# Packing products set one by one between the products of a half chunk

## The chip, the cores and the metric

The kernel runs on one core of a Trainium2 chip. The metric is the device time of one execution in microseconds, as the median of several runs. The engines that matter here are TensorE (PE in the rows, PEld for its weight loads), VectorE (DVE), ScalarE (ACT), GpSimd (POOL) and the DMA queue of SyncE (SPq).

## The reference

A graph attention layer and a graph averaging layer run over the same dense 0/1 adjacency matrix of 8192 x 8192 int32, with 8192 rows of 128 features.

```
Wh = h @ W
e = (Wh @ a1)[:, None] + (Wh @ a2)[None, :]
e = where(e > 0, e, 0.2 * e);  e = where(adj > 0, e, -9e15)
h_prime = softmax(e, axis=1) @ Wh
x = layernorm(x + elu(h_prime))
x1 = adj @ x / deg
x = layernorm(x + concat([x1, x], 1) @ weight + bias)
```

## The kernel before, in words

**Layer 0** (attention) goes over 32 groups of 256 rows. The exponential of a leaky sum is split into two cases, positive and negative score, and each case is a 0/1 mask times a precomputed table (`factors`). So a group needs 64 column tiles x 2 row tiles x 2 cases = 256 matrix products of 128x128 (mask, fp8, loaded as weights) by 128x258 (factors, f16, streamed). A group's 64 column tiles are cut into eight halves `h` of 8 tiles. Two halves make a chunk `c`. `multiply(g, h)` issues the 32 products of a half: four accumulators `a` (row tile b = a // 2, case a % 2), 8 tiles `j` each.

**Masks.** ACT writes the level bytes of a half with 8 activations (`scores`, L476). DVE unpacks the adjacency bits of a chunk from `words` to `edge_ring` (`unpack`, L887 and L889), ANDs the level bytes (`negative`, L919) and XORs the edges (`positive`, L926, which counts up `mask_ok`). PE waits for `mask_ok` ahead of each half.

**Packing.** The int32 adjacency is read only once. While group g is multiplied, the adjacency of group g+1 arrives chunk by chunk in `adj_ring` (two slots of 2 MB), and `pack(c)` turns it into 16-bit words: 32 small products a chunk, each with a 128x128 weight load (the low bytes of one int32 tile, step of four bytes) and a stream of 8 columns (`pack_w`), into `pack_ps`. It counts up `packed`, on which ACT copies the words out (L453) and SyncE's queue starts the load of the chunk after next (L226). `packable` (waits for `adj_in` and `words_ok`) stands ahead of a chunk's second half already.

**Signals out of a half.** `mask_used` is counted up by the last product of a half (ACT may then rewrite the level slot, 8 slots; DVE the edge slot, 4 slots). `acc_done` is counted up by the last product of the first three accumulators in half 7. ACT then copies and scales the positive sums (L487), DVE adds the negative ones (L948; for the second row tile it waits for `mask_used` of half 7), and POOL, DVE and ACT turn the sums into rows: ACT's exponential (L492) stands behind the scores of half 4 of the next group, its `normalise` (L512) behind those of half 6.

**Order.** Nothing is scheduled automatically: every engine runs its instructions in program order and waits on semaphores written by hand. PE's groups 1 to 30 are one loop (`pe.Fori(1, NG - 1)`, L701), groups 0 and 31 are written out. Group 31 packs nothing.

**Layer 1** (L746, L760, L770) is a loop of the same kind at L786 without packing. Nothing of the change lies in it.

Of the kernel before, what the change touches and what calls it, by code (L numbers as in the profile page):

```python
# [27 lines left out]
F8 = mybir.dt.float8e4  # L28
# [3 lines left out]
P = 128  # L32
BITS = 16
WPT = P // BITS
TPG = 2
GROUP = TPG * P
WPG = TPG * WPT
UNIT = 16
HALF = 8
# [9 lines left out]
ADJ_SLOTS = 2  # L49
# [5 lines left out]
def adj_resnorm_kernel(nc, x, adj, w0, a0, w1, b1, consts, out):  # L55
# [17 lines left out]
    with ctx:  # L73
        def sb(name, shape, dt):
            return ctx.enter_context(nc.sbuf_tensor(name, shape, dt))

        def sem(name):
            return ctx.enter_context(nc.semaphore(name))
# [4 lines left out]
        adj_ring = sb("adj_ring", [P, ADJ_SLOTS, TPG, COLS], I32)  # L83
# [3 lines left out]
        pack_w = sb("pack_w", [P, WPT], BF16)  # L87
# [20 lines left out]
        s_col, t_col, t_big, e_col, f_col, u_col, v_col, y_col, uy_col, vy_col, e_den, f_den = \  # L108
            (cols[:, k, :] for k in range(12))
        t_max, _, wh_max, wh_one, neg_t, neg_ft, inv_wh, scale_e, ones, sum_x = (one[:, k:k + 1] for k in range(10))  # L110
        t_max, t_spread = top_low[:, 2:3], wide_one[:, 7:8]
        half_max, row_max, neg_max, half_sum, row_sum = (wide_one[:, a:b] for a, b in ((0, 2), (2, 3), (3, 4), (4, 6), (6, 7)))
# [28 lines left out]
        pack_ps = [ctx.enter_context(nc.psum_tensor(f"pack_ps{k}", [P, 512], F32)) for k in range(2)]  # L141
# [23 lines left out]
        packed, words_ok, unpacked = (sem(n) for n in "packed words_ok unpacked".split())  # L165
        score_ok, mask_ok, mask_used, acc_done, neg_ready = (sem(n) for n in "score_ok mask_ok mask_used acc_done neg_ready".split())
# [435 lines left out]
        def _(pe):  # L602
# [32 lines left out]
            def packable(g, c, first=False):  # L635
                pe.wait_ge(adj_in[c % ADJ_SLOTS], 16 * (UPG // ADJ_SLOTS * g + c // ADJ_SLOTS + 1))
                if not first:
                    pe.wait_ge(words_ok, UPG * g + c - 1)

            def pack(c):  # L640

                for j in range(UNIT):
                    for t in range(TPG):
                        low_bytes = adj_ring[:, c % ADJ_SLOTS, t, j * P:(j + 1) * P].bitcast(F8)\
                            .rearrange("p (c b) -> p c b", b=4)[:, :, 0]
                        words_t = pack_ps[c % 2][:, j * WPG:(j + 1) * WPG].rearrange("p (w t) -> p w t", t=TPG)[:, :, t]
                        m = pe.matmul(words_t, low_bytes, pack_w[:, :], start=True, stop=True)  # L647
                m.then_inc(packed, 1)

            turn_x(0)  # L650
            for k in range(NX):
                if k + 1 < NX:
                    turn_x(k + 1)
                make_wh(k)
                if k == NX - 2:
                    pe.wait_ge(pack_w_ok, 1)
                    packable(0, 0, first=True)
                    pack(0)
            pe.wait_ge(wh_ok, NX)
            pe.transpose(turn_ps[0][:, 0:P], cols[:, 0:2, :].rearrange("p k j -> p (k j)"), ident).then_inc(s_turned, 1)  # L660
            packable(0, 1, first=True)
            pack(1)
            pe.wait_ge(sum_xb_ok, 1)
            pe.matmul(turn_ps[1][:, 0:F], sum_xb, wq[:, 0:F], start=True, stop=True).then_inc(mean_made, 1)
            for c in range(2, UPG):
                packable(0, c)
                pack(c)

            def multiply(g, h, factors_in=False, first=False):

                pe.wait_ge(mask_ok, 8 * g + h + 1)
                pe.sem_inc(masks_there, 1)
                for a in range(2 * TPG):
                    b, neg = a // 2, a % 2
                    if factors_in and a < 2:
                        pe.wait_ge((e_low_ok, f_low_ok)[neg], h // 2 + 1)
                    if h == 0 and not first:
                        pe.wait_ge(neg_added if neg else pos_copied, TPG * (g - 1) + b + 1)
                        pe.sem_inc(sums_read, 1)
                    for j in range(HALF):  # L680
                        jj = h * HALF + j
                        mask = level_bytes[:, h % MASK_SLOTS, j, b, :] if neg else \
                            edge_bytes[:, (h // 2) % EDGE_SLOTS, (h % 2) * HALF + j, b, :]
                        m = pe.matmul(acc[a][:, 0:ROW], mask, factors[:, neg, jj, :],  # L684
                                      start=(jj == 0), stop=(jj == NJ - 1))
                    if h == 7 and a < 2 * TPG - 1:
                        m.then_inc(acc_done, 1)
                m.then_inc(mask_used, 1)

            def group(g, first=False, last=False):  # L690
                for c in range(UPG):
                    for h in (2 * c, 2 * c + 1):
                        if h % 2 and not last:
                            packable(g + 1, c)
                        multiply(g, h, first and h % 2 == 0, first)
                    if not last:
                        pack(c)

            pe.wait_ge(den_hi_ok, 4)
            group(0, first=True)  # L700
            with pe.Fori(1, NG - 1) as g:  # L701
                group(g)
            group(NG - 1, last=True)

            with pe.If(is_wide(pe) > 0):
# [13 lines left out]
                with pe.Fori(0, NJ) as i:  # L719
                    pe.wait_ge(w_exp, 2 * i + 2)  # L720
                    pe.wait_ge(w_hidden, i + 1)
                    for q in range(NX):
                        wide_turn(i, q)
                        pe.wait_ge(w_copied, NX * i + q + 3)
                        for j in range(XB):
                            m = pe.matmul(acc[0][:, 0:F], prob_t[q % 2][:, j * P:(j + 1) * P], wh_all[:, XB * q + j, :],
                                          start=(q == 0 and j == 0), stop=(q == NX - 1 and j == XB - 1))
# [448 lines left out]
```

## Time and profile before

| | |
|---|---|
| median of 3 runs | 1607.88 us (1607.56 to 1608.36) |
| the profiled execution: own time | 1608.12 us |
| its span, first to last instruction | 1606.3 us |
| PE busy | 1557.2 us, 97% of the span |
| ACT busy | 1002.7 us, 62% (nearly all in layer 0) |
| layer 0's large products (L684), first and last start | 54.5 and 1090.3 us |
| layer 1's large products (L746), first and last start | 1090.4 and 1596.0 us |

The span is shorter than the execution's own time by 1.8 us, which lie outside the first and last instruction. The profiled execution is 0.24 us above the median. A matrix product's record lasts longer than the distance to the next one's start, since products are pipelined: what one costs is read as the distance between starts, not as its mean duration. Lines named PEldq are PE's own sequencer (branches, register sums, semaphore instructions).

### The profile page before, as it was taken

Reading aid. Unit: us, or ns where it says so; the run is one execution under the profiler, and the core shown is the slowest. Engines: PE = TensorE matmul, PEld = TensorE weight load, DVE = VectorE, ACT = ScalarE, POOL = GpSimd, SP = SyncE. Lnnn points to the kernel's source line nnn. Section 1 sums busy time; section 2 is a strip of 40 time slices with the busy share of each in tenths; the row PEclk is TensorE's granted clock in tenths of the full one; section 3 lists DMA queues with packets and bytes.
Section 4 is the critical chain, followed back from the end, with each engine's and each line's share of the span. In section 5 each row is a group of like instructions: output and inputs, shape, how many; then the busy total and the mean of one; then the engine's idle time right before and its main releaser. Section 6 shows DMA issues by size and latency. Waiting matters only on the chain. (4 is left out here: it accounts for less than half of the span.)

```text
span 1606.3 us, 46438 instructions
## 1 busy us (share of the span) xinstructions
PE 1557.2 (97%) x16966; PEld 1372.1 (85%) x16966; DVE 871.3 (54%) x3335; ACT 1002.7 (62%) x2513; POOL 437.4 (27%) x571
## 2 busy tenths in 40 slices
PE   7599999999999999999999999999999999999998
PEld 6488888888888888888888888887888888888886
DVE  7965555555555555555555555554444445454443
ACT  3999899989998999899988998881100000010000
POOL 0033443344334433443344334430000000000000
PEclk9799999999999999999999999999999999999999
DMA  8668777777777777777777777742000000000000
GB/s 272 237 258 280 274 274 283 278 274 274 280 280 276 274 276 275 285 274 274 280 282 271 273 286 278 270 136 64 20 16 16 16 16 16 16 19 17 16 16 16
DMA packets 100733, 302.84 MB, mean 189 GB/s; under 512 B 5729, under 2 KB 67937, under 8 KB 67937
## 3 DMA queue, kind: packets, MB, share of 16 engines
q1 hardware_dynamic: 100704, 302.48, 52.9%
q8 instruction: 16, 0.26, 0.1%
q14 instruction: 13, 0.10, 0.0%
HBM read 289.77 MB, written 12.68 MB: 188 GB/s over the span
## 5 line engine op out<-in xcount | busy, mean ns | idle before, releaser
L476 ACT ACTIVATE level_ring<-s_row,cols 128x256 fp8e4<-128x256 f32 x2048 | 839.3, 498 | 0.0
L684 PE MATMUL acc<-factors,edge_ring 128*128 128x258 f16 x4096 | 541.7, 273 | 17.7 <-issue 11.9
L684 PE MATMUL acc<-factors,level_ring 128*128 128x258 f16 x4096 | 541.1, 273 | 0.0
L746 PE MATMUL acc<-factors,adj_ring 128*128 128x258 f16 x4096 | 471.1, 274 | 3.6 <-DMA factors<-x_parts 3.0
L684 PEld LDWEIGHTS acc<-factors,edge_ring 128*128 128x128 fp8e4 x4096 | 390.8, 98 | 75.8 <-issue 20.0
L746 PEld LDWEIGHTS acc<-factors,adj_ring 128*128 128x128 fp8e4 x4096 | 400.5, 98 | 63.2 <-DMA factors<-x_parts 3.3
L684 PEld LDWEIGHTS acc<-factors,level_ring 128*128 128x128 fp8e4 x4096 | 399.6, 98 | 59.4
L919 DVE TENSOR_TENSOR level_ring<-level_ring,edge_ring 128x1024 uint16<-128x1024 uint16 x256 | 176.8, 692 | 237.7 <-ACT level_ring L476 226.8
L584 ACT ACTIVATE part_sums<-acc 128x258 f32<-128x258 f32 x32 | 12.4, 386 | 295.2 <-PE acc L746 295.2
L926 DVE TENSOR_TENSOR edge_ring<-edge_ring,level_ring 128x1024 uint16<-128x1024 uint16 x256 | 181.3, 739 | 0.0
L358 POOL TENSOR_SCALAR one<-mv 128x2 f32<-128x2 f32 x64 | 24.7, 387 | 549.4 <-DVE mv L971 549.4
L887 DVE TENSOR_SCALAR edge_ring<-words 128x256 uint16 (+1 forms) x896 | 160.3, 246 | 0.5 <-issue 0.5
L647 PEld LDWEIGHTS pack_ps<-pack_w,adj_ring 128*128 128x128 fp8e4 x4096 | 121.1, 97 | 16.4 <-DMA adj_ring<-in_adj 12.7
L647 PE MATMUL pack_ps<-pack_w,adj_ring 128*128 128x8 bf16 x4096 | 121.1, 169 | 12.5 <-DMA adj_ring<-in_adj 12.5
L887 DVE TENSOR_SCALAR adj_ring<-words 128x256 uint16 (+1 forms) x896 | 131.6, 215 | 1.1 <-DMA x_rows<-rows_y 1.1
L366 POOL TENSOR_TENSOR row_sums<-row_sums 128x258 f32<-128x258 f32 x31 | 21.4, 691 | 385.5 <-DVE row_sums L948 385.5
L592 ACT ACTIVATE level_ring<-turn_ps 128x512 f32<-128x512 f32 x32 | 19.1, 597 | 114.7 <-PE turn_ps L760 114.7
L1031 DVE TENSOR_TENSOR rows_y<-turn_ps,rows_y 128x256 f32<-128x256 f32 x32 | 13.6, 425 | 139.3 <-PE turn_ps L770 139.3
L948 DVE SCALAR_TENSOR_TENSOR row_sums<-acc,cols,part_sums 128x258 f32<-128x258 f32 x64 | 30.9, 485 | 87.0 <-ACT part_sums L487 58.0
L964 DVE BATCH_NORM_STATS2 stats<-rows_y 128x6 f32<-128x128 f32 x128 | 31.1, 285 | 84.2 <-POOL rows_y L395 83.1
L377 POOL TENSOR_SCALAR row_sums<-row_sums,one 128x128 f32<-128x128 f32 x62 | 71.7, 1160 | 11.9 <-DVE one L959 11.9
L412 POOL TENSOR_TENSOR parts<-row_sums,parts 128x256 f16<-128x256 f32 x31 | 37.5, 1209 | 89.3 <-ACT parts L500 89.3
(101 smaller groups left out, 840.4 us busy)
## 6 DMA issues: line engine op xcount, KB each, us to landing
adj_ring<-in_adj SPq DMA_DIRECT2D x128, 2048.0 KB, 7.7
x_parts<-parts SPq DMA_DIRECT2D x32, 129.0 KB, 4.8
factors<-x_parts SPq DMA_DIRECT2D x8, 516.0 KB, 3.9
factors<-in_x SPq DMA_DIRECT2D x8, 512.0 KB, 7.2
s_row<-s_and_t SPq DMA_DIRECT2D x32, 128.0 KB, 4.5
rows_x<-in_x SPq DMA_DIRECT2D x32, 128.0 KB, 4.5
x_rows<-rows_y SPq DMA_DIRECT2D x32, 128.0 KB, 7.9
rows_x<-x_rows SPq DMA_DIRECT2D x32, 128.0 KB, 2.1
```

The source lines that it names most:

```text
L358: pool.tensor_scalar(var_eps, mv[:, :, 1], EPS, None, ALU.add).then_inc(var_sem, TPG)
L377: pool.tensor_scalar(hidden[:, b, :], hidden[:, b, :], inv_den[:, b:b + 1], wh_one, ALU.mult, ALU.mult).then_inc(hidden_ok, 1)
L412: pool.tensor_tensor(parts[:, :, FD:FD + F], scaled, parts[:, :, 0:F], ALU.subtract).then_inc(low_part, 1)
L476: a = act.activation(level_bytes[:, h % MASK_SLOTS, j, :, :], s_halves[:, slot, :, :], ACT.Relu, bias=t_big[:, h * HALF + j:h * HALF + j + ...
L647: m = pe.matmul(words_t, low_bytes, pack_w[:, :], start=True, stop=True)
L684: m = pe.matmul(acc[a][:, 0:ROW], mask, factors[:, neg, jj, :], start=(jj == 0), stop=(jj == NJ - 1))
L746: m = pe.matmul(acc[b][:, 0:ROW], ring_1_bytes[:, c, j, b, :], factors[:, 0, jj, :], start=(jj == 0), stop=(jj == NJ - 1))
L887: d = dve.tensor_scalar(to, src, 6 - k, EDGES, ALU.logical_shift_left, ALU.bitwise_and)
L919: dve.tensor_tensor(level, level, edge_ring[:, c % EDGE_SLOTS, k * HALF:(k + 1) * HALF, :], ALU.bitwise_and).then_inc(neg_ready, 1)
L926: dve.tensor_tensor(edges, edges, level_ring[:, (2 * c + k) % MASK_SLOTS, :, :], ALU.bitwise_xor)\
L948: dve.scalar_tensor_tensor(out=row_sums[:, b, :], in0=acc[2 * b + 1][:, 0:ROW], scalar=v_col[:, bass.ds(TPG * g + b, 1)], in1=part_sums[:, ...
L964: d = dve.bn_stats(stats[:, b, :], rows_y[:, b, :])
```

## The change

`pack_tile(c, i)` issues packing product i of a chunk. In layer 0's groups, `multiply` of a chunk's second half gets `pack_chunk` and issues one packing product behind each of its 32 products. The separate `pack(c)` behind the half is gone there. (It stays ahead of the groups, for the chunks of group 0.) Counts, operands, waits and the loop are the same. `acc_done` and `mask_used` still hang on the same products, `packed` on the last packing product.

```diff
+            def pack_tile(c, i):
+
+                j, t = i // TPG, i % TPG
+                low_bytes = adj_ring[:, c % ADJ_SLOTS, t, j * P:(j + 1) * P].bitcast(F8)\
+                    .rearrange("p (c b) -> p c b", b=4)[:, :, 0]
+                words_t = pack_ps[c % 2][:, j * WPG:(j + 1) * WPG].rearrange("p (w t) -> p w t", t=TPG)[:, :, t]
+                return pe.matmul(words_t, low_bytes, pack_w[:, :], start=True, stop=True)
...
-            def multiply(g, h, factors_in=False, first=False):
+            def multiply(g, h, factors_in=False, first=False, pack_chunk=None):
...
-                    if h == 7 and a < 2 * TPG - 1:
-                        m.then_inc(acc_done, 1)
-                m.then_inc(mask_used, 1)
+                        if h == 7 and a < 2 * TPG - 1 and j == HALF - 1:
+                            m.then_inc(acc_done, 1)
+                        if a == 2 * TPG - 1 and j == HALF - 1:
+                            m.then_inc(mask_used, 1)
+                        if pack_chunk is not None:
+                            w = pack_tile(pack_chunk, a * HALF + j)
+                if pack_chunk is not None:
+                    w.then_inc(packed, 1)
...
-                        multiply(g, h, first and h % 2 == 0, first)
-                    if not last:
-                        pack(c)
+                        multiply(g, h, first and h % 2 == 0, first, c if h % 2 and not last else None)
```

PE at the end of the loop over groups, before: the last two accumulators of half 7 (L684), the packing block (L647), the loop's register sum and branch (L701), and then group 31.

```order
124 L684 MATMUL acc<-factors,edge_ring 128x258 x8
125 L684 MATMUL acc<-factors,level_ring 128x258 x8
126 L647 MATMUL pack_ps<-pack_w,adj_ring 128x8 x32
127 L701 REGISTER_ALU
128 L701 COMPARE_AND_BRANCH
129 L684 MATMUL acc<-factors,edge_ring 128x258 x8
```

The same place in the changed kernel (its loop is L708, its products L688 and L646):

```order
595 L688 MATMUL acc<-factors,level_ring 128x258
596 L646 MATMUL pack_ps<-pack_w,adj_ring 128x8
597 L688 MATMUL acc<-factors,level_ring 128x258
598 L646 MATMUL pack_ps<-pack_w,adj_ring 128x8
599 L708 REGISTER_ALU
600 L708 COMPARE_AND_BRANCH
601 L688 MATMUL acc<-factors,edge_ring 128x258 x8
```

What stands ahead of the branch was 32 small products. It is now a pair pattern of one large and one small product, which reaches back over the whole half.

PE inside a group, from the end of the first chunk to the second, before (L671 is the register sum ahead of the wait for `mask_ok`):

```order
89 L684 MATMUL acc<-factors,level_ring 128x258 x8
90 L647 MATMUL pack_ps<-pack_w,adj_ring 128x8 x32
91 L671 REGISTER_ALU
92 L684 MATMUL acc<-factors,edge_ring 128x258 x8
```

The same place in the changed kernel:

```order
384 L688 MATMUL acc<-factors,level_ring 128x258
385 L646 MATMUL pack_ps<-pack_w,adj_ring 128x8
386 L675 REGISTER_ALU
387 L688 MATMUL acc<-factors,edge_ring 128x258 x8
388 L688 MATMUL acc<-factors,level_ring 128x258 x8
389 L688 MATMUL acc<-factors,edge_ring 128x258 x8
390 L688 MATMUL acc<-factors,level_ring 128x258 x8
391 L675 REGISTER_ALU
392 L688 MATMUL acc<-factors,edge_ring 128x258
393 L646 MATMUL pack_ps<-pack_w,adj_ring 128x8
```

The block between the halves is gone, and the first half of the next chunk follows at once. The small products come back with its second half.

## Rows read from the trace of the kernel before

**Rows 1.** The page: busy time of each engine, share of the span

```profile
PE 1557.2 (97%) x16966; PEld 1372.1 (85%) x16966; DVE 871.3 (54%) x3335; ACT 1002.7 (62%) x2513; POOL 437.4 (27%) x571
```

**Rows 2.** Windows, 300 to 500 us: busy us (count) by engine, clock, DMA share, GB/s

```profile
core 0: us, PE busy (x) PEld busy (x) DVE busy (x) ACT busy (x) POOL busy (x), PEclk, DMA share, GB/s
...
300.00:500.00 200.00, 198.41 (x2392) 175.23 (x2390) 109.52 (x350) 180.20 (x460) 81.47 (x101) 1.00 0.76 277
```

**Rows 3.** Waits, 100 to 1040 us: us in total, times, longest us

```profile
ACT part_sums L492 <- POOL part_sums L381: 53.0, 30, 1.9
ACT rows_y L512 <- POOL one L403: 24.3, 29, 1.2
ACT part_sums L487 <- PE acc L684: 15.2, 28, 0.6
PE acc L684 <- issue: 7.7, 29, 0.3
```

**Rows 4.** Timeline of PE: a chunk's end, a group's end, the next

```profile
504.31 1.05 PE L684 MATMUL acc<-factors,level_ring 128*128 128x258 f16 x8
505.21 0.94 PE L647 MATMUL pack_ps<-pack_w,adj_ring 128*128 128x8 bf16 x32
506.01 1.05 PE L684 MATMUL acc<-factors,edge_ring 128*128 128x258 f16 x8
...
512.27 1.05 PE L684 MATMUL acc<-factors,level_ring 128*128 128x258 f16 x8
513.16 0.94 PE L647 MATMUL pack_ps<-pack_w,adj_ring 128*128 128x8 bf16 x32
514.37 1.06 PE L684 MATMUL acc<-factors,edge_ring 128*128 128x258 f16 x8 [0.27 <-issue]
...
538.22 1.05 PE L684 MATMUL acc<-factors,edge_ring 128*128 128x258 f16 x8
...
546.58 0.61 PE L684 MATMUL acc<-factors,edge_ring 128*128 128x258 f16 x4 [0.27 <-issue]
```

**Rows 5.** The loop's sequencer instructions (L701), 513 to 515 us

```profile
L701 PEldq ALU_OP  x1: 32/32/32, 513.5 to 513.5; - x1
L701 PEldq COMPARE_BRANCH  x1: 208/208/208, 513.6 to 513.6; - x1
```

**Rows 6.** Layer 1's loop branch, and the chain around it

```profile
L786 PEldq COMPARE_BRANCH  x1: 208/208/208, 1406.6 to 1406.6; - x1
```

```profile
1401.52 10.72 PE acc L746 x96
```

**Rows 7.** Timeline of PE at the end of group 0

```profile
86.56 0.94 PE L647 MATMUL pack_ps<-pack_w,adj_ring 128*128 128x8 bf16 x32
87.43 1.05 PE L684 MATMUL acc<-factors,edge_ring 128*128 128x258 f16 x8
...
94.58 0.94 PE L647 MATMUL pack_ps<-pack_w,adj_ring 128*128 128x8 bf16 x32
95.53 1.05 PE L684 MATMUL acc<-factors,edge_ring 128*128 128x258 f16 x8
```

**Rows 8.** All packing products, 100 to 1040 us: busy by window; durations min/median/max ns

```profile
100.00:1040.00 940.00, 110.57 (x3744) 110.62 (x3744) 41.98 (x116) 1.00 0.77 276
```

```profile
L647 PEld LDWEIGHTS pack_ps<-pack_w,adj_ring x3744: 95/97/98, 102.6 to 1037.7; 128*128 128x128 fp8e4 x198
L647 PE MATMUL pack_ps<-pack_w,adj_ring x3744: 169/169/171, 102.7 to 1037.7; 128*128 128x8 bf16 x198
```

**Rows 9.** Timeline of ACT and DVE around the group's end and its masks

```profile
512.57 0.47 ACT L487 ACTIVATE part_sums<-acc,cols 128x258 f32<-128x258 f32 x1 [0.58 <-PE acc L684]
513.47 0.48 DVE L948 SCALAR_TENSOR_TENSOR row_sums<-acc,cols,part_sums 128x258 f32<-128x258 f32 x1 [0.74 <-PE acc L684]
518.40 1.29 DVE L926 TENSOR_TENSOR edge_ring<-edge_ring,level_ring 128x1024 uint16<-128x1024 uint16 x2
521.46 0.42 ACT L492 ACTIVATE part_sums<-part_sums 128x256 f32<-128x256 f32 x1 [1.77 <-POOL part_sums L381]
529.36 0.88 ACT L512 ACTIVATE rows_y<-rows_y,one 128x128 f32<-128x128 f32 x2 [0.81 <-POOL one L403]
534.14 1.77 DVE L926 TENSOR_TENSOR edge_ring<-edge_ring,level_ring 128x1024 uint16<-128x1024 uint16 x2
```

**Rows 10.** DMA issues: count, KB each, median us from issue to landing

```profile
adj_ring<-in_adj SPq DMA_DIRECT2D x128, 2048.0 KB, 7.7
```

More of the change, by code:

```diff
@@ L638, in packable @@
                     pe.wait_ge(words_ok, UPG * g + c - 1)
-            def pack(c):
[L642 to L647, printed above, removed]
+            def pack_tile(c, i):
[4 more added lines that the diff above has]
+                return pe.matmul(words_t, low_bytes, pack_w[:, :], start=True, stop=True)
+            def pack(c):
+                for i in range(UNIT * TPG):
+                    m = pack_tile(c, i)
                 m.then_inc(packed, 1)
```

## The prediction

> **What bounds the kernel now.** I read the page first, then the windows, the waits, the timeline of PE and last the sequencer's own instructions. PE is busy for 97% of the span [rows 1]. In layer 0's steady stretch, 300 to 500 us, it is busy for 198.41 of 200 us at a granted clock of 1.00 (2.4 GHz), and ACT for 180.20 us [rows 2]. The reader is to see that the table of waits has just one entry for PE there: "issue", 29 times, 0.3 us at most [rows 3]. PE never waits for a mask or for the adjacency, so layer 0 lasts as long as PE's own sequence.
>
> That sequence reads off the timeline. Eight large products take 505.21 - 504.31 = 0.90 us (0.112 each). The 32 packing products of a chunk take 506.01 - 505.21 = 0.80 us, 25 ns each. At the end of a group the same block takes 514.37 - 513.16 = 1.21 us [rows 4], 0.41 more. The profile shows only 0.27 us of this as idle, because the records of the last small products stretch into it. A group lasts 546.58 - 514.37 = 32.21 us [rows 4].
>
> **The 0.41 us at a group's end.** The branch back lies there. The sequencer runs ahead of the array: its first loop instruction stands at 513.5 and the branch at 513.6, lasting 208 ns [rows 5], while packing products start until 513.16 + 31 x 0.025 = 513.94. The sequencer had all 32 handed over by 513.5, with (513.94 - 513.5) / 0.025 = about 17 of them still to start. From there to the first product of the next group it needs 514.37 - 513.5 = 0.87 us (branch, register sums, semaphores). The 17 small products cover 0.43 us of this, and the rest is the gap. Layer 1's loop has the same branch, with the same 208 ns, at 1406.6. It lies within 96 large products that run for 10.72 us without a break, 112 ns each [rows 6]. So a back edge costs nothing where large products are queued ahead of it.
>
> **The change part by part.**
>
> *The gap.* Now 17 products of the alternating pattern stand ahead of the branch. A pair lasts at least 0.112 + 0.025 = 0.137 us, so 17 cover 8.5 x 0.137 = 1.16 us, against the 0.87 needed. The gap should close: 29 back edges x 0.41 = 11.9 us. Group 0 is written out, but it shows small gaps of the same kind behind two blocks: 0.87 - 0.80 = 0.07 us and 0.95 - 0.80 = 0.15 us [rows 7]. Both should close as well. Together 12.1 us. If the queue held fewer mixed products than small ones, the cover would shrink: it falls to 0.87 at 13 products. Nothing in the rows says that it depends on the mix.
>
> *The small product's own slot.* No product is added or taken away, and what can change is only what a neighbour costs. The block is entered and left at the ordinary price: large to small 0.90 us for eight, small to large within 0.80 us for 32 [rows 4]. So a mask load behind a small product fits in its 25 ns, and a packing load fits behind a large product. The alternation is made of these two transitions, and they add up to the old price.
>
> One small thing speaks against exactly zero. The 117 packing blocks of 100 to 1040 us are busy for 110.57 us, 0.9450 us each. Less the last record (0.169) that leaves 0.776 us for 31 distances, 1 ns more than 31 x 25 [rows 8]. I put this 1 ns on the first small product, the one with a large product ahead of it. If it is a price of that transition, it now falls due at every pair: 31 groups x 4 chunks x 32 = 3968 products, of which 124 pay already, so 3844 x 1 ns = 3.8 us. The start times are rounded to 10 ns, so from them alone a transition could cost anything from 0 to 10 ns. I take 1 ns, since it comes from the mean over 117 blocks. The bounds are 0 (the excess is spread over the block) and 2 ns (the mask load's two-byte step costs as much again), 0 to 7.7 us.
>
> The Trainium skill, TensorE: Matmul & The Clock Gate, section "LDWEIGHTS (loading the stationary operand)", gives a weight load as its columns divided by 1.2 GHz. For 128 columns that is an estimate of 107 ns. By it a mask load that can only begin behind a small product would stick out by 82 ns, and the sum would be 3968 x 82 ns = 325 us slower. The trace disagrees: loads and small products run every 25 ns here [rows 4, 8]. The same page, section "Wait — 56ns, not 53.3ns?", has starts never nearer than about 25 ns however few the columns; by that the small product keeps its 25 ns wherever it stands, and the sum would be the 12.1 us alone.
>
> *The signals.* A half with packing lasts 4.38 instead of 3.58 us, and its last large product now stands 0.03 us ahead of the chunk's end instead of 0.8. Measured from the group's end, `acc_done` and `mask_used` of half 7 come up to 0.78 us later, and with the closed gap about 1.2 us later relative to the start of the next group. Behind them wait ACT's copy (it waits 0.58 us now), DVE's sum, and over POOL ACT's exponential (1.77 us) and `normalise` (0.81 us) [rows 9]. What stands behind these on ACT are the scores of halves 3 to 7, which DVE turns into the masks that PE needs. The tightest is half 6: its mask is ready at about 534.14 + 0.9 = 535.0, and PE begins that half at 538.22 [rows 4, 9], 3.2 us later. Less 1.2 us it is 2.0 us. The mask of half 2 is ready at about 519.0 and needed at 522.3. So PE still doesn't wait.
>
> ACT must also keep up with a shorter group. It is busy for 180.20 / 200 x 32.21 = 29.0 us of a group [rows 2] and waits for 0.58 + 1.77 + 0.81 us. The first two waits hang on the group's end and are slack, while the third follows from ACT's own exponential. So it needs 29.8 us or a little more, against a new group of 31.8. The adjacency load takes 7.7 us [rows 10] and is issued on `packed`, a chunk and a first half (8.0 + 3.6 us) ahead of its need, as before. Price of both: nothing. If the 2.0 us were gone, each us short would cost 30 us over the groups and show as PE waiting for DVE.
>
> **The sum.** 1608.12 - 12.1 + 3.8 = 1599.8 us for the profiled execution. The median of the runs is 0.24 us lower, so 1599.6. With 0 and 2 ns per pair it is 1595.8 and 1603.5.
>
> **The rivals.**
>
> *The alternation costs more than its two transitions (slower).* No row shows a mask load that follows a small product which itself follows a large one. The large product's last columns may still hold the array when that load begins. At 12.1 us / 3844 = 3.1 ns per pair it eats the gain. At 10 ns, the bound that the rounded start times leave, it gives 1607.9 - 12.1 + 38.4 = 1634 us. Against it stands the first packing product of each block, whose successor's load is in that very place and costs 1 ns. Chance 0.13, and 0.10 for the stretch of 2 to 3.9 ns in between, 1603.5 to 1611.
>
> *The gap stays (the change does not do that).* The branch might wait for something that long products don't cover, or the queue might hold fewer of the mixed ones. Then the time is 1607.9 plus the pair price, 1608 to 1612. Layer 1's branch speaks against it. Chance 0.06.
>
> *The small products hide (much faster).* If 25 ns is a matter of rate that long products even out, a small product costs only its 8 columns: at 112 ns for 258 columns 3.5 ns, say 8 with an overhead. PE would save 3968 x 17 = 67 us more. ACT would then bind: its 29.8 us a group allow 30 x 2.4 = 72 us in all, hence 1536 to 1545 us, or any part of that. Against it: the product behind a block starts after the same 25 ns, though by then nothing small follows. Chance 0.05.
>
> **How the numbers follow.** The forecast, 1595.5 to 1603.5, has 0.66. I predict 1599.6 us with a range of 1590 to 1608. It reaches a little below the forecast's own range, for a product that hides in part, and takes in most of the stretch between. About this measurement's bound of 0.2% (3.2 us): faster by more is below 1604.7, slower above 1611.1. The forecast and the hiding give 0.71, and the nearer part of the stretch 0.05: faster 0.76. The rest of the stretch and most of the staying gap: same 0.10. Slower 0.14.
>
> **What would show it.** In the changed profile PE's 29 waits for "issue" are gone, and a group lasts 31.8 us plus 0.13 for each ns of the pair price. A second half lasts 4.38 to 4.45 us. Starts in it lie 112 and 25 or 26 ns apart. Layer 1 keeps its length. ACT's waits grow at L487 to about 1 us and shrink nowhere by more than the group does. The prediction is wrong if a pair lasts over 140 ns, if PE waits for DVE's masks in the loop, or if the issue gaps are still there.

## The result: 17.4 us less, and the profile after

| | before | changed |
|---|---|---|
| median | 1607.72 us (1606.16 to 1608.36, 4 runs) | 1590.33 us (1587.96 to 1592.57, 4 runs) |
| profiled execution, span | 1606.3 us | 1586.1 us |

The ratio is 0.9893, with a 95% interval of 0.9876 to 0.991. The direction was forecast, and the time lies just inside the range. The gain is twice the forecast one: 17.4 instead of 12.1 - 3.8 = 8.3 us. The profiled execution is the fastest of the four, 2.4 us under the median.

The page of the changed kernel, busy time by engine:

```profile
PE 1544.6 (97%) x16966; PEld 1369.4 (86%) x16966; DVE 871.8 (55%) x3335; ACT 999.9 (63%) x2513; POOL 437.1 (28%) x571
```

Its waits, PE, 1040 to 1072 us (us in total, times, longest):

```profile
PE acc L688 <- DVE edge_ring L933: 0.8, 1, 0.8
```

The same window as [rows 2], and the whole loop, in which PE is busy without a break:

```profile
300.00:500.00 200.00, 200.00 (x2431) 178.22 (x2430) 111.33 (x352) 183.29 (x470) 81.80 (x101) 1.00 0.77 281
100.00:1040.00 940.00, 940.00 (x11424) 837.69 (x11421) 526.17 (x1667) 860.59 (x2201) 389.39 (x477) 1.00 0.78 281
```

PE is busy for 200.00 of 200 us where it was 198.41 [rows 2], and the 29 waits for "issue" [rows 3] are gone. The timeline of PE, to be laid beside [rows 4] (start, length, count; from the plain half to the alternating one, and over the group's end):

```profile
498.56 1.05 PE L688 MATMUL acc<-factors,edge_ring 128*128 128x258 f16 x8
...
502.14 0.27 PE L688 MATMUL acc<-factors,edge_ring 128*128 128x258 f16 x1
502.25 0.17 PE L646 MATMUL pack_ps<-pack_w,adj_ring 128*128 128x8 bf16 x1
502.27 0.27 PE L688 MATMUL acc<-factors,edge_ring 128*128 128x258 f16 x1
502.38 0.17 PE L646 MATMUL pack_ps<-pack_w,adj_ring 128*128 128x8 bf16 x1
502.41 0.27 PE L688 MATMUL acc<-factors,edge_ring 128*128 128x258 f16 x1
...
506.44 0.17 PE L646 MATMUL pack_ps<-pack_w,adj_ring 128*128 128x8 bf16 x1
506.47 1.05 PE L688 MATMUL acc<-factors,edge_ring 128*128 128x258 f16 x8
...
538.07 1.05 PE L688 MATMUL acc<-factors,edge_ring 128*128 128x258 f16 x8
```

The loop's branch stands here between the rows (L708):

```profile
L708 PEldq COMPARE_BRANCH  x1: 208/208/208, 505.4 to 505.4; - x1
```

Three things are to be seen. The branch at 505.4 lies within the alternating products, and the next group begins at 506.47, 0.03 us behind the last small product: no gap. A plain half lasts 502.14 - 498.56 = 3.58 us, as before. But the half with packing lasts 506.47 - 502.14 = 4.33 us, 135.3 ns a pair, where two unchanged neighbours would give 136.8 and the forecast had 137.8. A group lasts 538.07 - 506.47 = 31.60 us instead of 32.21.

That makes 0.61 us a group: 0.41 from the back edge, 0.20 from the pairs. The starts of single products in the trace, which the timeline rounds, show where these 0.20 come from. From 100 to 1040 us a large product in plain order (large ones ahead of it and behind it) starts 109.2 ns ahead of the next if its tile number j is a multiple of 4 and 112.6 ns if not, 111.75 on average. In the changed kernel a large product between two small ones takes 109.15 ns whatever its j is (3687 of them), and a small one 26.0. A pair is 135.2 ns instead of 111.75 + 25.0.

### The profile page after: what moved, and what is told of

Same layout as the page of the kernel before. It is cut to its first block and busy times, and to the rows that moved or that the text cites. A ratio compares the mean times of both kernels' runs of the same rounds, so it can differ in the third digit from the quotient of the medians.

```text
span 1586.1 us, 46438 instructions
## 1 busy us (share of the span) xinstructions
PE 1544.6 (97%) x16966; PEld 1369.4 (86%) x16966; DVE 871.8 (55%) x3335; ACT 999.9 (63%) x2513; POOL 437.1 (28%) x571
## 5 line engine op out<-in xcount | busy, mean ns | idle before, releaser
L688 PE MATMUL acc<-factors,edge_ring 128*128 128x258 f16 x4096 | 581.8, 272 | 11.0 <-DVE edge_ring L933 6.6
L688 PE MATMUL acc<-factors,level_ring 128*128 128x258 f16 x4096 | 581.4, 272 | 0.0
L646 PE MATMUL pack_ps<-pack_w,adj_ring 128*128 128x8 bf16 x4096 | 544.8, 170 | 11.9 <-DMA adj_ring<-in_adj 11.9
L688 PEld LDWEIGHTS acc<-factors,edge_ring 128*128 128x128 fp8e4 x4096 | 387.6, 97 | 66.0 <-issue 11.9
L688 PEld LDWEIGHTS acc<-factors,level_ring 128*128 128x128 fp8e4 x4096 | 396.4, 97 | 55.7
L646 PEld LDWEIGHTS pack_ps<-pack_w,adj_ring 128*128 128x128 fp8e4 x4096 | 387.8, 97 | 14.1 <-DMA adj_ring<-in_adj 12.2
L584 ACT ACTIVATE part_sums<-acc 128x258 f32<-128x258 f32 x32 | 12.4, 387 | 294.2 <-PE acc L753 294.2
L366 POOL TENSOR_TENSOR row_sums<-row_sums 128x258 f32<-128x258 f32 x31 | 21.5, 692 | 368.6 <-DVE row_sums L955 368.6
```

The costliest lines, as they stand in the source:

```text
L646: return pe.matmul(words_t, low_bytes, pack_w[:, :], start=True, stop=True)
```

## The experiments

All ran with 3 or 5 rounds beside the kernel before. Its median was 1608.84 us in the first set, 1608.29 in the second and 1608.69 in the third. Single executions of one kernel lie up to 3 us off their median, and this goes with the granted clock of the whole execution: of the kernel before, in the first set, the six with 0.986 took 1610.6 to 1611.9 us and the two with 0.990 took 1605.9 and 1606.2. So the length of a group, read from two starts of PE's timeline where the clock is 1.00, is the sharper figure. A median of a few executions can be a microsecond or two off for this reason.

**The gap alone.** The kernel before, with the last chunk's block ahead of the last eight large products.

```diff
                     for j in range(HALF):
+                        if pack_last and a * HALF + j == 2 * TPG * HALF - 8:
+                            pack(UPG - 1)
...
-                        multiply(g, h, first and h % 2 == 0, first)
-                    if not last:
+                        multiply(g, h, first and h % 2 == 0, first, h == 7 and not last)
+                    if not last and c < UPG - 1:
                         pack(c)
```

> The kernel before, with one edit: the packing block of a group's last chunk stands ahead of the last eight large products of half 7 instead of behind them. No alternation. Theory 1 (two separate effects: the gap at the back edge closes as soon as long products are queued ahead of the branch; the alternation is priced by itself): the 29 waits for issue vanish, a group lasts 32.21 - 0.41 = 31.80 us, and the time is 1607.7 - 12.1 = 1595.6 us. Rival (the whole gain of the change comes from the alternation, and the gap closes only with it): 1607.7 us with the gap still there.

1596.57 us (ratio 0.9928, 0.9915 to 0.9941), a group of 31.80 us. The timeline of PE shows the block and a seamless group's end:

```profile
510.13 0.95 PE L647 MATMUL pack_ps<-pack_w,adj_ring 128*128 128x8 bf16 x32
510.93 1.06 PE L686 MATMUL acc<-factors,level_ring 128*128 128x258 f16 x8
511.83 1.06 PE L686 MATMUL acc<-factors,edge_ring 128*128 128x258 f16 x8
```

The gap closes without any alternation, and the rival falls. By the medians it is worth 12.3 us. That this meets the expected 12.1 so closely is partly chance: groups 1 to 30 are 12.1 us shorter together, but group 31 has a new wait of 0.8 us:

```profile
1074.92 1.05 PE L686 MATMUL acc<-factors,edge_ring 128*128 128x258 f16 x8 [0.83 <-DVE edge_ring L928]
```

**How long the cover must be.** The same with `- 2` in place of `- 8`.

> As the kernel with the moved block, but the block stands ahead of the last two large products of half 7 only. Theory 1 (what counts is how long the about 17 products queued ahead of the branch last, against the 0.87 us that the sequencer needs): 2 x 0.112 + 15 x 0.025 = 0.60 us of cover, so 0.27 us of the 0.41 remain, a group lasts 32.07 us, and the time is 1607.7 - 29 x 0.14 = 1603.6 us. Rival (the gap hangs on the branch standing directly behind small products): closed, 1595.6 us.

1603.96 us (0.9976, 0.9965 to 0.9986), groups of 32.04 to 32.13 us.

```profile
512.27 0.38 PE L686 MATMUL acc<-factors,level_ring 128*128 128x258 f16 x2
512.73 1.06 PE L686 MATMUL acc<-factors,edge_ring 128*128 128x258 f16 x8
```

The two large products need 0.22 us and the next group begins after 0.46, so 0.24 us of the gap are left. Expected were 0.27. It is the length of what is queued ahead of the branch that counts.

**The alternation alone.** The changed kernel, with the last chunk in a block behind its half.

```diff
-                        multiply(g, h, first and h % 2 == 0, first, c if h % 2 and not last else None)
+                        multiply(g, h, first and h % 2 == 0, first, c if h % 2 and not last and c < UPG - 1 else None)
+                    if not last and c == UPG - 1:
+                        pack(c)
```

> The changed kernel, with the last chunk of each group packed in a block behind its half again, so the gap at the back edge should be back and only the alternation of chunks 0 to 2 is left. Theory 1 with the distances of the changed kernel's trace (a large product behind a small one 109.2 ns instead of a mean of 111.75, a small one behind a large one 26.0 instead of 25.0, together 1.6 ns less per pair): 31 x 3 x 32 = 2976 pairs x 1.6 ns = 4.8 us, so 1602.9 us, and a group of 32.21 - 0.15 = 32.06 us. Rival (the prediction's +1 ns per pair): 1610.7 us. Rival (the alternation is what gave all 17 us): 1595 us.

1605.09 us (0.9976, 0.9967 to 0.9985), 3.8 us less than before, and a group of 515.34 - 483.25 = 32.09 us. The gap is back:

```profile
483.25 1.08 PE L688 MATMUL acc<-factors,edge_ring 128*128 128x258 f16 x8 [0.27 <-issue]
...
515.34 1.08 PE L688 MATMUL acc<-factors,edge_ring 128*128 128x258 f16 x8 [0.27 <-issue]
```

96 pairs a group save 0.12 us, 1.3 ns each, a little under the 1.6. Its single starts show the rest: in 27 of the groups one large product near the start takes 146 ns, which costs 0.03 us a group. The kernel before has only two such products in all, of 140 and 146 ns. The prediction's +1 ns is refuted: its 1610.7 us lies outside all runs of this kernel.

**The alternation in the last chunk only**, chunks 0 to 2 in blocks.

```diff
+                        multiply(g, h, first and h % 2 == 0, first, c if h == 7 and not last else None)
+                    if not last and c < UPG - 1:
+                        pack(c)
```

> The changed kernel with only the last chunk of each group alternating; chunks 0 to 2 are packed in a block behind their second half, as before. Theory (gap and alternation add up): the gap is closed, 0.41 us a group, and 32 pairs save 1.6 ns each, 0.05 us a group: a group of 31.75 us, and in all 12.1 + 1.6 = 13.7 us less than the kernel before. Rival (the alternation saves nothing by itself): 31.80 us.

1597.40 us (0.9933, 0.9919 to 0.9946), a group of 508.98 - 477.22 = 31.76 us, against 31.75 expected. By the medians it is 11.3 us under the kernel before, not the 13.7 expected. The group fits. The expectation lacked the wait in group 31, which is there in this kernel too:

```profile
1071.23 1.05 PE L688 MATMUL acc<-factors,edge_ring 128*128 128x258 f16 x8 [0.78 <-DVE edge_ring L935]
```

Layer 0, from its first large product to its last, is 12.4 us shorter than before (54.9 to 1078.3 us). Expected less the new wait were 12.9. The rest of the difference is within the scatter.

**The change once more, on the chip of the kernel above.**

> The changed kernel itself once more, on the same chip as the kernel with only the last chunk alternating and those with four packing products together. Expected 17 to 18 us below the kernel before, a group of 31.60 us, and 4 to 5 us below the kernel that alternates in the last chunk alone. If the first measurement was helped by its other chip, it is off by more than 3 us.

1591.21 us (0.9896, 0.9881 to 0.9912), 17.5 us under the kernel before, 6.2 under the one above, a group of 506.59 - 474.99 = 31.60 us. The first measurement stands.

**Two by two.** Which of a large product's neighbours counts?

```diff
-                        if pack_chunk is not None:
-                            w = pack_tile(pack_chunk, a * HALF + j)
+                        if pack_chunk is not None and j % 2:
+                            for i in (j - 1, j):
+                                w = pack_tile(pack_chunk, a * HALF + i)
```

> The changed kernel, with two packing products behind every second large product instead of one behind each. The gap stays closed (12.1 us). Theory 1a (only a large product that directly follows a small one is shorter, because something of its start is hidden in the small one's 25 ns): of four large products one more than in plain order is short, 109.2 instead of 112.5, against two transitions at +1 ns, 0.34 ns less per pair, 1.3 us: 1594.3 us. Theory 1b (a large product is shorter if a small one stands on either side of it): all are short, 2 ns less per pair, 8 us: 1587.6 us. Prediction's theory (no large product gets shorter, +0.5 ns per pair): 1597.6 us.

1598.13 us (0.9935, 0.9923 to 0.9948), a group of 510.98 - 479.19 = 31.79 us. The single starts: a large product with a small one ahead of it takes 109.2 ns (1890 of them), though half of them are j = 2 or 6, which take 112.5 in plain order; one with a small product behind it 112.6 (1891). So what stands ahead counts, as in theory 1a. The small products cost more here, 26.4 ns behind a large one and 25.2 behind a small one, so almost nothing of the gain is left: 31.79 us against the 31.80 of a block. The median lies 3.8 us above 1a's 1594.3, beside the prediction's 1597.6. The time alone would not have told the two apart, the starts do.

**Four by four, at two places.** The pair of kernels differs only in where the four small products stand: behind j = 3 and 7 (a row with j a multiple of 4 follows) or behind j = 1 and 5 (j = 2 or 6 follows).

```diff
+                        if pack_chunk is not None and j % 4 == 3:
+                            for i in range(4):
+                                w = pack_tile(pack_chunk, a * HALF + j // 4 * 4 + i)
```

and with `j % 4 == 1`.

> The changed kernel with four packing products together behind every fourth large product, so that the large product behind them is always one whose factors row begins at a multiple of 16 bytes. Theory (a small product ahead hides the extra of a row off 16 bytes, and here there is none to hide): nothing is saved, and 8 instead of 1 transitions a chunk cost 1 ns each: a group of 31.80 + 4 x 7 x 0.001 = 31.83 us. Rival (any small product ahead shortens the large one, or breaking up the row of large products does): as many are shortened as in the kernel with the other place, 31.73 us in both.

> The same counts and the same alternation of four and four, but set off by two large products: behind each four small ones stands a large product whose row begins 8 bytes off a multiple of 16. Theory: each of these 8 a chunk is 3.3 ns shorter, 32 x 3.3 = 0.107 us a group: 31.83 - 0.107 = 31.73 us, and 0.107 x 31 = 3.3 us less in all than with the other place. Rival (the place of the row plays no part): no difference between the two.

Ahead of j = 0 and 4: 1600.75 us (0.9949, 0.9934 to 0.9964).

```profile
481.46 1.05 PE L688 MATMUL acc<-factors,edge_ring 128*128 128x258 f16 x8
...
513.32 1.05 PE L688 MATMUL acc<-factors,edge_ring 128*128 128x258 f16 x8
```

Ahead of j = 2 and 6: 1594.54 us (0.9912, 0.9896 to 0.9927).

```profile
479.76 1.06 PE L688 MATMUL acc<-factors,edge_ring 128*128 128x258 f16 x8
...
511.51 1.06 PE L688 MATMUL acc<-factors,edge_ring 128*128 128x258 f16 x8
```

The groups last 31.86 and 31.75 us. The difference of 0.11 us a group is the expected 0.107. A small product ahead shortens just those large ones that are long in plain order. The medians differ by 6.2 us, more than the 3.3 of the groups, but so do the granted clocks (0.987 to 0.989 in the four executions of the first, 0.988 to 0.991 in the second). The two profiled executions, both at 0.988, took 1601.08 and 1597.81 us, 3.3 apart.

**The rows' place in memory.** The factors' rows are 258 f16 numbers, 516 bytes apart, so only every fourth begins at a multiple of 16 bytes. The kernel before, with rows 264 numbers (528 bytes) apart:

```diff
+    ROWP = 264
...
+        factors = sb("factors", [P, 2, NJ, ROWP], F16)
...
+                        m = pe.matmul(acc[a][:, 0:ROW], mask, factors[:, neg, jj, 0:ROW],
```

The x1 parts (`parts`, `parts_dram`) are widened alike. `w1_sb` and `bias_row` are loaded into `s_row` once layer 0 is over, and PE's wait for `w1_sb` moves behind layer 1's first group.

> The kernel before, with the rows of the factors 264 numbers (528 bytes) apart instead of 258 (516 bytes), so that every streamed row begins at a multiple of 16 bytes; 258 are still streamed. To make room, the second layer's weights and bias are loaded later into the space of s_row. Theory A (in plain order three of four large products start 112.5 ns and one 109.2 ns ahead of the next, since three of four rows begin off 16 bytes; a small product ahead hides the difference): all large products of both layers take 109.2 ns, 12288 x 2.6 ns = 32 us less, 1575.8 us, with the gap at the back edge still there; a group lasts 31.55 us. Theory B (the pattern of four comes from the order of loads or of the accumulator, not from the rows' place): 1607.7 us.

1588.31 us (0.9878, 0.9861 to 0.9895). A group lasts 31.77 us (892.58 to 924.35), with the gap still in it:

```profile
892.58 0.93 PE L685 MATMUL acc<-factors,edge_ring 128*128 128x258 f16 x7 [0.27 <-issue]
...
924.35 0.82 PE L685 MATMUL acc<-factors,edge_ring 128*128 128x258 f16 x6 [0.27 <-issue]
```

The chain in layer 1, beside the 10.72 us of [rows 6]:

```profile
1214.13 10.56 PE acc L747 x96
```

The mechanism holds (the pattern of four is gone, all are 110.0 ns), but its size was taken too high: where all rows are aligned, one costs 110.0 in plain order and not 109.15, so 1.75 ns are saved on average and not 2.6. 12288 x 1.75 ns = 21.5 us; measured were 20.0.

**Half of the rows aligned.** The same with rows 520 bytes apart (`ROWP = 260`).

> As the padded kernel before, but with rows 260 numbers (520 bytes) apart: every second row begins at a multiple of 16 bytes. Theory A (16 bytes decide): every second large product is short, a mean of 110.8 instead of 111.75 ns, 12288 x 0.85 ns = 10.4 us: 1597.3 us. If a multiple of 8 bytes were enough: all short, 1575.8 us. If the later loads or the space alone did something, it would show here and in the other padded one alike. Theory B: 1607.7 us.

1601.05 us (0.9954, 0.9941 to 0.9968). The chain in layer 1:

```profile
1207.89 10.65 PE acc L747 x96
```

96 products last 10.72, 10.65 and 10.56 us with a quarter, half and all of the rows at a multiple of 16 bytes. It is the 16 bytes, not eight, and not the later loads, which both padded kernels have. Nor are 32 bytes needed: with rows 528 bytes apart only every second begins at a multiple of 32, and all take 110.0 ns. The median fell by 7.2 us and not by the expected 10.4. Of layer 0's products in plain order those with an even j take 109.2 ns and those with an odd one 112.6 to 112.8.

**The changed kernel, padded**, to 528 bytes.

> The changed kernel with the same padding. Theory A: only the 12288 - 3968 = 8320 large products that have no small one ahead of them can still gain, 8320 x 2.6 ns = 21.6 us: 1590.3 - 21.6 = 1568.7 us. The alternation then costs 1 ns a pair over a block, so the distance to the padded kernel before is 12.1 - 3.9 = 8.2 us, the figure of the prediction, and not 17. Theory B: 1590.3 us.

1577.95 us (0.9815, 0.9802 to 0.9828), a group of 504.12 - 472.76 = 31.36 us. Against the padded kernel before that is 10.4 us and 31.77 - 31.36 = 0.41 us a group: the gap and nothing else. Expected were 1568.7 us and 8.2 us between the two. Both missed because they rest on 109.2 ns for every aligned row: in plain order it is 110.0, so the padding saves less, and a small product ahead still shortens the large one by 0.8 ns. With aligned rows the alternation gives nothing (109.2 + 25.9 a pair against 110.0 + 25.0).

**Padded, with the moved block**, no alternation.

> Padding to 528 bytes together with the packing block ahead of the last eight large products, no alternation: the best that theory A and the gap give. 1575.8 - 12.1 = 1563.7 us, some 4 us below the padded changed kernel, since a block saves the 1 ns a pair. A group would last 31.55 - 0.41 = 31.14 us, against about 29.8 that ACT needs. Rival (with shorter groups ACT or the masks bind): a group stays above 31.3 us and PE shows waits for DVE inside the loop.

1576.18 us (0.9806, 0.979 to 0.9821), groups of 31.36 to 31.41 us. It beats both kernels of the study, and so does the padded changed one; between these two the intervals overlap. Neither forecast of a 4 us distance nor 1563.7 us held, since both rested on 109.2 ns for an aligned row. PE has no wait for DVE inside the loop, only one of 1.3 us in the last group.

## Why the prediction was right in its sign and wrong in its size

**The gap at the back edge: right.** 0.41 us at 29 edges, closed by long products queued ahead of the branch. Shown by the moved block (a group of 31.80 us, as expected) and by the one with half a cover (0.24 us left against 0.27).

**The small product's own slot: this step failed.** The prediction said that the alternation "is made of these two transitions, and they add up to the old price", plus 1 ns a pair. That 1 ns is real: in the trace before, the first small product of a block takes 26.1 ns, and in the changed kernel every one takes 26.0. The missing term is the large product behind a small one. In the trace before, the only such product is the first behind each block, and it is always j = 0, whose 109 ns is its ordinary price. So the transition looked free, though it shortens the three others of each four, by 3.4 ns. Over a pair that is 2.6 less and 1.0 more, -1.6 ns instead of +1.0. Times 3968 pairs it is -6.3 us instead of +3.8.

**The sum again.** 12.1 + 6.3 = 18.4 us. Off this come 0.8 us in group 31, which the sum lacked. It packs nothing and so would last 28.6 us on PE, less than the 29.8 that ACT needs for a group with packing. PE waits there for the masks of half 6 (the row of waits above), and the DVE instruction ahead of these had waited for ACT's level bytes:

```profile
1064.15 0.69 DVE L926 TENSOR_TENSOR level_ring<-level_ring,edge_ring 128x1024 uint16<-128x1024 uint16 x1 [4.64 <-ACT level_ring L476]
1066.07 1.05 PE L688 MATMUL acc<-factors,edge_ring 128*128 128x258 f16 x8 [0.80 <-DVE edge_ring L933]
```

The two kernels with a moved block have the same wait (0.83 and 0.81 us), the kernel before has none there. So it comes with the later end of half 7, not with the alternation. That leaves 17.6 us, against 17.4 and 17.5 by the medians. Layer 0 by itself says the same: its large products start from 54.5 to 1090.3 us before and from 54.7 to 1073.1 us in the changed kernel, 17.4 us less.

The spans of the two profiled executions differ by more, 20.2 us. The further 3 us are no gain of the change. They lie in layer 1, whose large products take 502.6 us from first to last instead of 505.6. At its start PE waits for `x_parts` in both, but the granted clock behind the longer wait is lower (the first two lines are of the kernel before):

```profile
1105.96 6.24 PE L746 MATMUL acc<-factors,adj_ring 128*128 128x258 f16 x29 [3.01 <-DMA factors<-x_parts]
1100.00:1120.00 20.00, 16.99 (x128) 13.76 (x126) 5.83 (x37) 1.37 (x3) 0.00 (x0) 0.83 0.19 50
```

```profile
1088.64 6.43 PE L753 MATMUL acc<-factors,adj_ring 128*128 128x258 f16 x56 [1.99 <-DMA factors<-x_parts]
1080.00:1100.00 20.00, 18.01 (x162) 15.66 (x160) 6.27 (x38) 2.67 (x6) 0.43 (x2) 1.00 0.20 54
```

The products behind the wait show it as well: 56 take 6.43 us in the changed kernel, and 29 take 6.24 us in the kernel before, where they would take some 3.4 at a clock of 1.00.

**The signals: right for the masks, wrong for one wait.** Within the loop PE never waits for DVE. ACT's exponential starts 514.75 - 506.47 = 8.28 us behind the new group's start (before 521.46 - 514.37 = 7.09), the 1.2 us later that was forecast. But ACT's wait at L487 did not grow to 1 us, it vanished. ACT comes to that copy, still busy with its scores, some 0.3 us after the sums are there (its two copies start at 505.44 and 505.80, and the last product of the sums ends at 505.52). That this is ACT taking up the shorter group is argued, not shown:

```profile
505.44 0.82 ACT L487 ACTIVATE part_sums<-acc,cols 128x258 f32<-128x258 f32 x2
...
514.75 0.42 ACT L492 ACTIVATE part_sums<-part_sums 128x256 f32<-128x256 f32 x1 [1.84 <-POOL part_sums L381]
```

**The rivals.** That the alternation costs more, and that the gap stays, are refuted. That small products hide is refuted in its form: a small product still has its 26 ns. What hides is a part of the large one behind it.

**Still open** is what the 3.4 ns are. The place of the row decides over them and a small product ahead hides them, but no run shows by what path. Nor does one show why an aligned row takes 110.0 ns in a row of such, but 109.15 behind a small product or behind rows off 16 bytes.

## What to carry to other kernels

In these runs a loop's back edge on TensorE costs nothing if the products queued ahead of it (here some 17) run longer than the branch and the first instructions behind it need (here 0.87 us). Put long products there and not a block of short ones.

Let the rows that TensorE streams begin at a multiple of 16 bytes. Here six unused numbers a row gave about as much as the change under study (20.0 against 17.4 us; the intervals overlap), and what the alternation itself gained, some 6 of the 17.4 us, was only that it hid the fault.

Before two transitions of a trace are added up for a new order, look whether the products in them stand for all: here the one witness was the first of four kinds.

Before two profiled executions are subtracted, look at the granted clock of each stretch: here 3 of 20.2 us came from it and not from the change.

## What the runs showed of the hardware

- A streamed product of 258 f16 columns with a large one ahead of it starts 109.2 to 110.0 ns ahead of the next if its row begins at a multiple of 16 bytes, and 112.4 to 112.9 ns if it begins 4, 8 or 12 bytes off. In both layers, at 2.4 GHz (granted clock 1.00).
- A product of 8 columns directly ahead takes away the difference, one directly behind does not (109.2 against 112.6 ns).
- A product of 8 columns behind a large one takes 25.9 to 26.5 ns, behind its like 25.0 to 25.2. With all rows aligned, the first of a block took 28.4.
- Behind a wait of 3.01 us at the start of layer 1 the granted clock was 0.83 on average over 20 us, behind one of 1.99 us it was 1.00.
